# A decoder kernel: the value sums of two heads in one strip of 32 rows, and a new step table

## The reference

```
scores = einsum("bhqd,bhkd->bhqk", qh, kh) * scale
attn = softmax(scores, axis=-1)
out = einsum("bhqk,bhkd->bhqd", attn, vh)
out = out.transpose(0, 2, 1, 3).reshape(B, S, E)
y = out @ Wo
```

## Time and profile before

| | us |
|---|---|
| median of 3 runs | 1210.09 (1208.85 to 1210.41) |
| the profiled execution's own time | 1201.47 |
| its span, first to last instruction | 1199.6 |
| TensorE matmul busy | 1106.6 (92%) |
| VectorE busy | 911.0 (76%) |
| ScalarE busy | 700.7 (58%) |
| GpSimd busy | 332.1 (28%) |

### The profile page before, as it was taken

The page is one execution under the profiler, slowest core; times in us unless marked ns, Lnnn a source line. Parts: engine busy times, 40 slices in busy tenths (PEclk is TensorE's granted clock), DMA queues, the critical chain, the costliest instruction groups (busy, mean ns, idle before and its releaser), DMA issues. The chain is left out here.

```text
span 1199.6 us, 24688 instructions
## 1 busy us (share of the span) xinstructions
PE 1106.6 (92%) x8142; PEld 699.3 (58%) x8153; DVE 911.0 (76%) x2363; ACT 700.7 (58%) x1532; POOL 332.1 (28%) x443
## 2 busy tenths in 40 slices
PE   7878988899999999999998999988989999999997
PEld 2233545458667775677554454654657676765576
DVE  6999697778788889657788872427798999876654
ACT  4443678775545458775565545436575665558552
POOL 4546223002211111011223323030474454421001
PEclk9988699899999999999999999999999999999999
DMA  7003224222323222033524414120100010132012
GB/s 243 1 0 106 80 86 164 65 72 73 105 63 103 82 86 66 33 94 119 147 81 164 156 72 161 52 70 25 44 19 2 1 34 26 58 121 86 16 52 70
DMA packets 75787, 93.01 MB, mean 78 GB/s; under 512 B 6537, under 2 KB 60273, under 8 KB 73841
## 3 DMA queue, kind: packets, MB, share of 16 engines
q1 hardware_dynamic: 74640, 89.34, 23.3%
q0 software_dynamic: 1024, 2.10, 0.6%
HBM read 64.25 MB, written 28.67 MB: 77 GB/s over the span
## 5 line engine op out<-in xcount | busy, mean ns | idle before, releaser
L1420 ACT ACTIVATE P<-bank 128x512 f32<-128x512 f32 (+1 forms) x448 | 230.6, 585 | 92.8 <-PE bank L1116 91.3
L1832 DVE TENSOR_REDUCE mx<-bank 128x2 f32<-128x512 f32 x320 | 200.7, 683 | 24.7 <-PE bank L1087 22.9
L1633 POOL TENSOR_SCALAR rstd<-mv 128x2 f32<-128x2 f32 x56 | 15.0, 268 | 414.0 <-DVE mv L1684 335.2
L1129 PE MATMUL bank<-P,V 128*32 128x256 f32 (+1 forms) x1536 | 101.0, 386 | 3.1 <-ACT P L1420 1.9
L1233 PE MATMUL bank<-room 128*128 128x256 f32 x384 | 97.2, 389 | 2.1 <-DVE room L1980 2.1
L1227 PE MATMUL bank<-xT,room 128*128 128x256 f32 x384 | 95.6, 387 | 0.0
L1087 PE MATMUL bank<-QKR 48*128 48x256 bf16 (+1 forms) x896 | 82.8, 276 | 11.4 <-DMA QKR<-split_rows 7.2
L1116 PE MATMUL bank<-QKR 50*128 50x256 bf16 (+1 forms) x896 | 85.0, 274 | 5.5 <-DMA QKR<-msT 2.1
L1233 PEld LDWEIGHTS bank<-room 128*128 128x128 f32 x384 | 69.8, 191 | 18.2 <-issue 6.0
L1980 DVE TENSOR_TENSOR room<-room 128x512 f32<-128x512 f32 x96 | 63.4, 700 | 21.8 <-DMA room<-gate_rows 21.1
L1227 PEld LDWEIGHTS bank<-xT,room 128*128 128x128 f32 x384 | 69.4, 190 | 13.7 <-issue 5.6
(11 more groups left out here) (288 smaller groups left out, 2421.7 us busy)
## 6 DMA issues: line engine op xcount, KB each, us to landing
QKR<-split_rows SPq DMA_DIRECT2D x112, 192.0 KB
room<-gate_rows SPq DMA_DIRECT2D x48, 256.0 KB, 3.6
split_rows<-parts SPq DMA_DIRECT2D x56, 192.0 KB, 2.4
split_rows<-parts SPq DMA_DIRECT2D x56, 128.0 KB, 2.0
room<-in_w SPq DMA_DIRECT2D x6, 1024.0 KB
room<-in_w SPq DMA_DIRECT2D x3, 2048.0 KB
split_rows<-parts SPq DMA_DIRECT2D x56, 64.0 KB, 1.7
room<-in_mask SPq DMA_DIRECT2D x4, 512.0 KB, 7.9
```

Of the source, the lines that this page charges most:

```text
L1129: last = nc.tensor.matmul(bk[32 * j:32 * j + 32, q0:S], V[:, n % 2, t, 4 * g + j, :], P[:, (e - 1 + j) % NBUF_P, t * S:t * S + S - q0], st ...
L1420: nc.scalar.activation(P[:, (e - 1) % NBUF_P, 0:width], psum(st, p)[:, 0:width], ACT.Exp, scale=SCALE).then_inc(read[k], 1)
L1832: V_.reduce_max(to, sc[:, :].rearrange("p (t s) -> p t s", t=TPB), AX.X).then_inc(read[k], 1)
```

## The change

- `V` keeps its shape, but the heads of slots 8 to 15 have their values in columns 16 to 23 and their one in column 24, zeros elsewhere. The host reorders the columns of the value weights (`VALUE_HEAD`) and the rows of the output weights (`OUT_HEAD`).
- `PV` with its four groups becomes `PA` and `PV`, with two each. `PA` writes four heads (columns 0 to 15 of each strip) into a bank, `PV` adds four more heads to the same bank (columns 16 to 31). Only `PV` has an ACT copy behind it. The bank is held from `PA` until that copy.
- `OT` comes once per unit: four transpositions for both tiles of tokens, one reciprocal of 32 sums and one product of 256 columns.
- `V`'s two DVE operations split by half of the heads in place of by tile of tokens.
- In the planner, `HOP` goes from 0.15 to 0.2, a change between bf16 steps (`NARROW`) and others is charged (0.09 and 0.04), and some costs are set anew. `ORDER` is found anew for the new steps. The waits for a bank that `STAT` empties count the emptyings in `STAT`'s order.

```diff
+VALUE_HEAD = [SLOT_HEAD[8 * r + 4 * half + j] for half in range(2) for r in range(2) for j in range(4)]
+OUT_HEAD = [SLOT_HEAD[8 * r + 4 * half + j] for r in range(2) for j in range(4) for half in range(2)]
...
-    "MX": ((ACT, 0.72),), "MB": ((PE, 0.24), (DVE, 2.34)), "MC": ...
+    "MX": ((ACT, 0.72),), "MB": ((PE, 0.24), (DVE, 2.48)), "MC": ...
-    "P2": ((PE, 0.27), (ACT, 0.95)), "PV": ((PE, 0.95), (ACT, 0.33)), "ZV": ((PE, 0.95), (DVE, 0.86)),
-    "OT": ((PE, 0.43), (DVE, 0.48)), "OX": ((PE, 0.27), (ACT, 0.33)), "Y": ((PE, 0.54),),
+    "P2": ((PE, 0.27), (ACT, 0.95)), "PA": ((PE, 0.95),), "PV": ((PE, 0.95), (ACT, 0.33)), "ZV": ((PE, 0.95), (DVE, 0.86)),
+    "OT": ((PE, 0.43), (DVE, 0.64)), "OX": ((PE, 0.27), (ACT, 0.33)), "Y": ((PE, 0.54),),
...
-HOP = 0.15
+HOP = 0.2
+NARROW = ("SM", "P2", "MT", "MB", "MC")
+TO_NARROW, TO_WIDE = 0.09, 0.04
...
+def weighing(a, b, g):
+    return ("PV" if g % 2 else "PA", a, b, g // 2)
...
-                                              else [("PV", a, b, g) for g in range(4)])])
+                                              else [(k, a, b, r) for r in range(2) for k in ("PA", "PV")])])
...
-                chain += [("OT", a, b, t) for t in range(TPB)] + [("OX", a, b), ("Y", a, b)]
+                chain += [("OT", a, b), ("OX", a, b), ("Y", a, b)]
...
 ORDER = (
-    "aaaaaaaababaccdebcbaeddacedbcaebaceddbabcebdaceaebcbddacedabcedbacebdcaedbcaebaecbdcaebdcaeddbacedaecebadecdcnbbonacebda"
+    "aaaaaaaababaccbebddacebaecbdaecdacbeddacebaebcdaceddbbaecacebbddaecaceddbabecacdedbbaecbdaecdacedbaceedbacebacdedbbaaecc"
...
-HELD_FOR = ("LN", "MN", "BI", "MY", "Y", "LY", "YT")
+HELD_FOR = ("PA", "LN", "MN", "BI", "MY", "Y", "LY", "YT")
...
-                elif k == "PV":
-                    _, a, b, g = st
-                    n, e = unit[(a, b)], exp_no[(a, b, 2 * g)]
-                    if g == 0:
+                elif k in ("PA", "PV"):
+                    _, a, b, r = st
+                    half = int(k == "PV")
+                    n, e = unit[(a, b)], exp_no[(a, b, 4 * r + 2 * half)]
+                    bk = psum(("PA", a, b, r))
+                    if r == 0 and half == 0:
                         finished(pe, ("V", a, b))
                     pe.wait_ge(read["P2"], e + 3)
...
-                            last = nc.tensor.matmul(bk[32 * j:32 * j + 32, q0:S], V[:, n % 2, t, 4 * g + j, :],
-                                                    P[:, (e - 1 + j) % NBUF_P, t * S:t * S + S - q0], start=(t == 0), stop=(t == TPB - 1), skip_group_check=True)
+                            last = nc.tensor.matmul(bk[32 * j:32 * j + 32, q0:S], V[:, n % 2, t, 8 * half + 4 * r + j, :],
+                                                    P[:, (e - 1 + j) % NBUF_P, t * S:t * S + S - q0], start=(half == 0 and t == 0), stop=(half == 1 and t == TPB - 1), skip_group_check=True)
...
-                    for g in range(4):
-                        last = nc.tensor.transpose(bk[:, g * 128:(g + 1) * 128], og[:, unit[(a, b)] % 2, g, t * 128:(t + 1) * 128], ident[:, :])
+                    for t in range(TPB):
+                        for r in range(2):
+                            last = nc.tensor.transpose(bk[:, (2 * t + r) * 128:(2 * t + r + 1) * 128], og[:, unit[(a, b)] % 2, r, t * 128:(t + 1) * 128], ident[:, :])
...
-                    nc.scalar.copy(og[:, n % 2, g, :], bk[:, 0:S]).then_inc(read[k], 1)
+                    nc.scalar.copy(og[:, n % 2, r, :], psum(("PA", a, b, r))[:, 0:S]).then_inc(read["PA"], 1)
...
-                    y = bk[:, :].rearrange("p (h c) -> p h c", c=32)
-                    link(V_.reciprocal(rden[:, t, :].unsqueeze(2), y[:, :, DH:DH + 1]))
+                    y = bk[:, :].rearrange("p (h c) -> p h c", c=16)
+                    shares = rden[:, :, :].rearrange("p t h -> p (t h)").unsqueeze(2)
+                    link(V_.reciprocal(shares, y[:, :, DH:DH + 1]))
...
-                    V_.tensor_tensor(o[:, t, :].rearrange("p (h d) -> p h d", d=DH), y[:, :, 0:DH],
-                                     rden[:, t, :].unsqueeze(2).to_broadcast([128, NH, DH]), ALU.mult).then_inc(read[k], 1)
+                    V_.tensor_tensor(o[:, :, :].rearrange("p t (h d) -> p (t h) d", d=DH), y[:, :, 0:DH], shares.to_broadcast([128, 2 * NH, DH]), ALU.mult).then_inc(read[k], 1)
```

More of the change, by code:

```diff
@@ L349, in needs @@
         if k == "V":
-            return ([("GM", b)] if a == GATHERED else x_of(SUB_OF[("attn", a)], b)) + [("PV", *at(j), 3) for j in range(n - 2, -1, -2) if at(j)[0] != SELF_WIDE][:1]
+            return ([("GM", b)] if a == GATHERED else x_of(SUB_OF[("attn", a)], b)) + [("PV", *at(j), 1) for j in range(n - 2, -1, -2) if at(j)[0] != SELF_WIDE][:1]
         if k == "SM":
@@ L458, in needs @@
         if r[0] == "lin":
-            return [("PV", MASKED, B - 1, 3), ("LW",), ("LD", "zero")]
-        return [("GM", r[1] - 1)] if r[1] else [("PV", MASKED, B - 1, 3)]
+            return [("PV", MASKED, B - 1, 1), ("LW",), ("LD", "zero")]
+        return [("GM", r[1] - 1)] if r[1] else [("PV", MASKED, B - 1, 1)]
     return []
@@ L522, in plan @@
                 in_table = table(st)
+            if eng == PE and narrow != (st[0] in NARROW):
+                t += TO_WIDE if narrow else TO_NARROW
+                narrow = not narrow
             t += dur
@@ L527, in plan @@
             until[at] = 1e9 if st[0] in HELD_FOR else t + HOP
-        if st[0] == "YC":
-            until[place[("BI", *st[1:]), 0]] = t + HOP
-        if st[0] == "MY" and st[1] % 2:
-            until[place[("MN", st[1] // 2), 0]] = t + HOP
-        if st[0] == "LR":
-            until[place[("LN", *st[1:]), 0]] = t + HOP
-        if st[0] == "STAT" and SUBLAYERS[st[1]] not in (("attn", SELF_WIDE), ("moe", DISPATCHED)):
-            until[place[stat_source(st), 0]] = t + HOP
+        if released_by(st):
+            until[place[released_by(st), 0]] = t + HOP
         done[st] = t + LANDING.get(st[0], HOP)
@@ L570, in decoder @@
     count, seen, held, latest = {}, {}, {}, {}
+    emptied, emptyings = {}, {}
     for st in steps:
+        if st[0] == "STAT" and released_by(st):
+            emptied[released_by(st)] = emptyings[released_by(st)[0]] = emptyings.get(released_by(st)[0], 0) + 1
         seen[st[0]] = seen.get(st[0], 0) + 1
@@ L804, in finished @@
         def finished(eng, st):
-            eng.wait_ge(read[st[0]], banks_of(st) * count[st])
+            eng.wait_ge(read[st[0]], emptied.get(st, banks_of(st) * count[st]))
         def full(eng, st):
@@ L995, in _ @@
                             old, nth = held[st, j]
-                            pe.wait_ge(read[old[0]], banks_of(old) * (count[old] - 1) + nth + 1)
+                            pe.wait_ge(read[old[0]], emptied.get(old, banks_of(old) * (count[old] - 1) + nth + 1))
                     bk = psum(st)
@@ L1673, in _ @@
             link(V_.memset(V[:, :, :, :, :], 0.0))
-            link(V_.memset(V[:, :, :, :, DH:DH + 1], 1.0))
+            for half in range(2):
+                link(V_.memset(V[:, :, :, 8 * half:8 * half + 8, 16 * half + DH:16 * half + DH + 1], 1.0))
             link(V_.memset(abar.rearrange("p i (b s) -> p i b s", s=S)[:, :, :, 0:1], 0.0))
@@ L1802, in _ @@
                     for j in [j for j in range(n - 2, -1, -2) if units[j][1] != SELF_WIDE][:1]:
-                        full(dve, ("PV", units[j][1], units[j][2], 3))
-                    for t in range(TPB):
-                        to, v = V[:, n % 2, t, :, 0:DH], bk[:, t * 128:(t + 1) * 128].rearrange("p (h d) -> p h d", d=DH)
+                        full(dve, ("PV", units[j][1], units[j][2], 1))
+                    for half in range(2):
+                        to = V[:, n % 2, :, 8 * half:8 * half + 8, 16 * half:16 * half + DH]
+                        v = bk[:, 0:S].rearrange("p (t q h d) -> p t q h d", t=TPB, q=2, d=DH)[:, :, half]
                         if a in BIASED:
-                            last = V_.tensor_tensor(to, v, bvo[:, BIASED[a], 0, :].rearrange("p (h d) -> p h d", d=DH), ALU.add)
+                            bias = bvo[:, BIASED[a], 0, :].rearrange("p (q h d) -> p q h d", q=2, d=DH)[:, half]
+                            last = V_.tensor_tensor(to, v, bias.unsqueeze(1).to_broadcast([128, TPB, 8, DH]), ALU.add)
                         else:
@@ L2074, in by_dim, with by_head @@
         return np.swapaxes(a.reshape(a.shape[:-1] + (2, NPAIR, DH)), -1, -2).reshape(a.shape)
-    def by_slot(a):
-        return a.reshape(a.shape[:-1] + (NH, DH))[..., SLOT_HEAD, :].reshape(a.shape)
-    attn = [[by_dim(x[0]), by_dim(x[1]), x[2] if n == SELF_WIDE else by_slot(x[2]), by_slot(x[3].T).T] for n, x in enumerate(attn)]
+    def by_head(a, order):
+        return a.reshape(a.shape[:-1] + (NH, DH))[..., order, :].reshape(a.shape)
+    attn = [[by_dim(x[0]), by_dim(x[1]), x[2] if n == SELF_WIDE else by_head(x[2], VALUE_HEAD), by_head(x[3].T, OUT_HEAD).T] for n, x in enumerate(attn)]
     mask = w["mask_Bx1xSxS2_ik1"][:, 0]
```

108 lines of the change are left out of this document (61 added, 47 removed).

## The result

The changed kernel takes **1166.1 us** (median of 4 runs, 1164.2 to 1168.7) against 1210.3 us for the kernel before in the same session: a ratio of 0.9634, 95% interval 0.9609 to 0.9659. I had forecast 1193 and a range down to 1176. On another chip the same pair gave 0.9689 (0.9642 to 0.9735). The direction was right; I had forecast 17 us less, and it is 37 to 44.

A forecast was written before the change was run, and what follows sets the result against it. TensorE's own work, in step-table order, was taken to set the pace (92% busy). Transpositions 11.8 plus turns 12 make 24 us, times 0.7 gives 17: 1201.5 to 1184.5, plus 8.6 carried over, 1193 us; range 1176 to 1208.

The forecast's parts named there:

- The rest of the table: Stages without attention: a new order with altered planner costs and nothing else, taken as 0 with 6 us either side.
- third rival: Table gains more than the removed work: an order avoiding the clock fall at 112 to 136 us, 1183 us; chance 0.16.
- TensorE's work: Work removed in the attention stages, transpositions plus turns: 24 us, or 18 us if turns hang on tile shape.
- The transpositions: Attention units: 24 lose one group of four transpositions each, at 0.49 us, 11.8 us of TensorE work.
- The turns: TensorE's step order: 72 fewer pairs of bf16/fp32 turns at 0.19 us, less 1.6 us back, together 12 us.
- the count by data type: Step tables: bf16 steps meeting any other, 576 times before and 432 after, the basis of the 12 us.
- the count by shape: Step tables: changes of tile shape, 810 before and 747 after, giving 6 us in place of 12.
- The conversion: Attention stages: share of removed TensorE work that comes out as time, 0.7 taken between 0.4 and 1.0.
- The changed instructions of ScalarE and VectorE: Attention units: 48 copies fewer, 18.2 us of ScalarE; VectorE 7.6 us less; both hidden behind TensorE, no time counted.
- the held bank: PSUM between `PA` and the copy behind `PV`: one of eight banks lost some 3 us, 48 times; taken as 0.
- the value sums: `PA` and `PV` matmuls: not removed, staying at 1536 records and 101 us.
- The 8.6 us carried over: Profiled execution before, 1201.5 us, lay 8.6 us under the median of 1210.1; added to 1184.5 to give 1193.

The follow-up runs named there:

- e13: Kernel before with only its step table searched on for 30 million moves, steps and planner constants unchanged: ratio 0.9814 to the kernel before.
- e17: Kernel before with only its step table searched on, old constants, from another random seed: ratio 0.9855 to the kernel before.
- e10: Changed kernel with each unit's transpositions issued four times, some 31 us of TensorE work added: ratio 0.9853 to the kernel before.
- e2: Kernel before, its steps kept, given the new step table and new planner constants: ratio 0.9773 to the kernel before, 27 us.
- e9: The changed kernel itself, nothing altered, timed again on a second chip: ratio 0.9689 to the kernel before.
- e5: Changed kernel with an isolated block of matmul groups, alone and in pairs of kinds, behind its last step: 0.19 to 0.36 us extra per shape-changing pair; no kernel time given.

## Why the prediction was wrong

- **What bounds the kernel.** "TensorE's own work sets the pace, and its order is the step table" was half right. At 92% busy its order mattered as well as its work: a better order of the same work gave 18 to 22 us (e13, e17), and 31 us of added work gave 20 (e10).
- **The step that failed** is "The rest of the table. I take 0 with 6 us to either side; a reason for a sign I do not see in the rows". The rows did show 93 us of idle TensorE, 15.8 of them in one attention stage, and I took the table as if it could only shift them. In their place the runs show that the new table with the old parts is worth 27 us (e2), and that in its profile 19.0 us are idle time of TensorE that went (93.0 to 74.0), a term that my sum doesn't have. My third rival named the table, at 0.16, with the clock as its mechanism. For the profiled executions that is not what happened: both have a mean granted clock of 0.976, and both 0.93 in the stage that holds the stretch that I had named. Over more runs the clock has a part in it: on the chip of e9 the kernel before had 0.965 to 0.975 in 11 runs and the changed one 0.972 to 0.986 in 6, which goes with 5 to 7 of the 39 us by the slope of the last section. So the rival was right on the table and wrong on most of the reason.
- **TensorE's work** as a whole was near: 24 us forecast, 18 by the count of shapes, 19.7 us less busy time measured.
- **The transpositions**, 11.8 us at 0.7: 8 us. Under the old table the parts gave 3 us, under the new one 0.9773 less 0.969 or so, 10 us with some 8 to either side, and with a table searched for each side 0 us (new constants) or 19 to 24 us (old constants). There is no one price; it hangs on what else sets the time.
- **The turns**, 12 us: the count by data type was wrong and the count by shape right, as the isolated block shows; and neither count orders the times, since the table with the most changes of shape, 855, is as fast as those with 734 and 747. Among the tables searched for the same steps, fewer turns do go with less busy time; for the new steps, what is saved there comes back as idle time. How much of the changed table's 27 us is turns and how much is waits, no run separates; its profile has 12.9 us less busy time and 19.0 us less idle time, at a clock of 0.982 against 0.976.
- **The conversion** of 0.7 is not refuted: 0.64 for 31 us of added work, and for the first 10 us anything from nothing to all of it, within the noise. It turned 24 us into 17; what the sum lacked were the waits. The table of cells does hint at a second limit: either the parts or the constants take TensorE's work down, and the second then finds little. The idle times, which rise again in the kernels with the least busy time, fit that. It is argued, not shown; what the other limit is stays open.
- **The changed instructions of ScalarE and VectorE, the held bank, the value sums**: as predicted, to within 6 ns an instruction and 1 us. ScalarE's busy time as a whole fell by 9.9 us and not by the 18.2 of the copies; why, I did not look into.
- **The 8.6 us carried over** from the profiled execution to the median held badly: the changed kernel's profiled execution is at its median. The runs of before on one chip go with the clock, 1192.7 us at 0.976 and 1204.7 us at 0.966, and the first profile, at 0.976, was near the top of that range: a lucky draw. So at equal clock the two kernels differ by 35 us, and some 9 of the 44 go with the lower clock that most runs of the kernel before have. That is a difference of the kernels too, if it is as steady as on the chip of e9; what causes it is not shown. On that second chip the difference of the medians was 39.
- **The direction** was right in part by luck: the parts, on which half of my sum stood, give 3 us under the old table, with zero inside the interval, and most of the gain came from a term that I had put at nothing.

## What to carry to other kernels

Where a hand-held or searched order drives all engines, ask first how far that order is from its own optimum: 30 million moves on the planner that is already there were worth 18 to 22 us, where the changed steps under the old table were worth 3. An ablation of parts under a table that was made for other parts measures the misfit; give each side its own table. And before an engine's removed work is turned into time, add the same work and look; add enough that it stands clear of the noise, as 31 us did here and 10 us did not, and read the granted clock and the idle time beside the time.

## What the runs showed of the hardware that I had not expected

A change of the tile's shape on TensorE and back costs 0.19 us between bf16 full and bf16 64-row tiles, 0.28 us between fp32 full and bf16 64-row ones and 0.36 us between fp32 full and fp32 64-row ones, and a change of data type at the same shape costs nothing measurable (e5). The mean granted clock of a run goes with its time: over 13 runs of the kernel before on one chip, 0.976 to 0.966 went with 1192.7 to 1204.7 us, 1%, and a line through all 13 gives about 9 us per 0.010. I had called 0.2% the resolution. Kernels are to be compared on one chip, over many runs, with their clocks beside the times; whether a kernel's order itself raises or lowers its clock, these runs don't show.
